# Moving the residual add of the combine stage from VectorE to GpSimd in an attention and mixture-of-experts kernel

## The chip, the cores and the metric

The kernel runs on one core of a Trainium2 chip. The metric is the device time of one execution in microseconds. Engines are called TensorE (PE in the profile, its weight load PEld), VectorE (DVE), ScalarE (ACT), GpSimd (POOL) and SyncE (SP, which here only issues DMAs).

## What is computed

One transformer layer on x of 4 x 2048 tokens by 512 features, float32:

```python
x = x + layernorm(attention(layernorm(x)))   # linear attention, 16 heads, random features
x = x + layernorm(ffn(layernorm(x)))         # 32 experts, 4 per token, plus a shared expert
```

The last line is where the change lies. For a token, ffn is the weighted sum of its experts' outputs plus the output of a shared expert, `silu(X @ sw1.T) * (X @ sw3.T) @ sw2.T`. That sum is normalised over the 512 features (mean 0, variance 1, epsilon 1e-5) and the residual, the x of the line above, is added.

## The kernel before

The 8192 tokens are worked on in NG = 16 groups of G = 512; a group is held as a tile of 128 partitions by A = 4 by 512 features. The stages follow each other: projection, sums over the sequence, attention with routing, experts, combine. The last three are in one block of programs (attend_route_and_expert_stage, line 1728), each engine with an instruction stream of its own, in order, tied to the others by semaphores. The change is in expert_and_combine_programs (line 1292).

**Experts.** For each of 32 experts GpSimd gathers rows by indirect DMA (L1412), TensorE turns them and does the two layers, VectorE weighs the result, and GpSimd adds it by indirect DMA into the sum acc in HBM (L1426).

**Combine.** It begins when the last of those additions has landed. The groups are taken in a written order, of which the text calls the places positions 0 to 15:

```python
ORDER = (2, 3, 4, 0, 5, 6, 7, 1, 8, 9, 10, 11, 12, 13, 14, 15)   # line 1301
```

Groups 0 and 1 (positions 3 and 7) had their shared expert done before the experts, so they have no matmuls here. For the others TensorE does, per group, up of the next group (L1485: two halves i, each eight matmuls into gates and eight into ups, 128x512) and then down of this group in four passes a (L1500, four matmuls each). Up of a half waits until VectorE has read the banks before (h_ready); down's first pass waits for both halves of low (low_ready); down's pass a waits until VectorE has taken the product of pass a-2 out of its PSUM bank (y_copied).

VectorE's order in a group at position q with matmuls (lines 1693 to 1721) is: make_shift of q-1 (L1663, waits for rstd_ready), hidden of the next group's half 0 (L1610: silu'd gate, from SBUF, times up, from PSUM), include 0 (L1642: down's product, from PSUM, plus the loaded sum, from SBUF), hidden half 1, measure 0 (L1651: statistics of one 128x512 tile), include 1, low half 0 (L1615: h minus its 16-bit part, both from SBUF), measure 1, include 2, low half 1, measure 2, include 3, **add of q-1 (L1670)**, measure 3, aggregate (L1656). At positions 3 and 7 it is make_shift, four measures, add, aggregate. "The first include" of a group is L1642 with a = 0.

ScalarE's order at q: silu of the next group's two halves (L1540), make_high of half 0 (L1546), scale of q-1 (L1552: four activations that normalise the sum in place, after the shift), make_high of half 1, store of q-1 (L1559, a DMA that waits for out_ready). GpSimd only makes rstd for each position: it adds epsilon (L1436) when the aggregate is there, and raises to the power -0.5 (L1438).

SyncE loads: load_acc of q (L1361) into one of ACCS = 5 buffers, where from q = 5 it waits for out_ready of q-5; load_x1 (L1354) into one of X1S = 5 buffers after their store; load_shared (L1348) after up of an earlier group.

add(q) waits for z_ready (scale of q done) and x1_loaded, adds the whole tile in one instruction of 128x2048, x1 + total into x1, and counts out_ready, for which the store and load_acc wait.

Elsewhere in the kernel, the profile's lines name L329 and L330 (memsets on GpSimd in the projection), L1251 and L1253 (GpSimd's add of epsilon and power in the attention stage), L1105 and L1101 (VectorE, 128x2048, both inputs in SBUF, in the attention stage).

Of the kernel before, what the change touches and what calls it, by code (L numbers as in the profile page):

```python
# [14 lines left out]
NG = T // G  # L15
# [12 lines left out]
ALU = mybir.AluOpType  # L28
# [1263 lines left out]
def expert_and_combine_programs(nc, io, keep, t, wait_routed, wait_slots):  # L1292

    with ExitStack() as tiles:
# [3 lines left out]
        XTS, X1S, ACCS = 8, 5, 5  # L1298
# [13 lines left out]
        x1 = [t.sb(f"x1{r}", [P, A, E]) for r in range(X1S)]  # L1312
        total = [y[0][:], y[1][:]] + [r[:].rearrange("p a n -> p (a n)").bitcast(F32).rearrange(
            "p (a e) -> p a e", a=A) for r in rows]
# [13 lines left out]
        x1_loaded, out_stored = ([t.sem(f"{n}{r}") for r in range(X1S)] for n in ("x1_loaded", "out_stored"))  # L1328
# [4 lines left out]
        stats_ready, mv_ready, var_ready, rstd_ready, shift_ready, z_ready, out_ready, power_ready = (  # L1333
            t.sem(n) for n in ("stats_ready", "mv_ready", "var_ready", "rstd_ready", "shift_ready", "z_ready",
                               "out_ready", "power_ready"))
# [67 lines left out]
        def pool_program(pool):  # L1403
            def gather(e):
                r = e % AHEAD
                pool.wait_ge(slot_loaded[e % RING], 16 * (e // RING) + 16)
                if e >= AHEAD:
                    pool.wait_ge(turned_ready, A * (e - AHEAD + 1))
                for a in range(A):
                    if e < AHEAD:  # L1410
                        pool.wait_ge(cleared, A * e + a + 1)
                    nc.gpsimd.indirect_dma_start(  # L1412
                        out=rows[r][:, a, :], out_offset=None, in_=io["rows"],
                        in_offset=bass.IndirectOffsetOnAxis(ap=slot[e % RING][:, a, 0:1], axis=0),
                        bounds_check=T - 1, oob_is_err=False).then_inc(gathered[r], 16)

            def add(e):

                if e == 0:
                    for k in range(2):  # L1420
                        pool.wait_ge(y_stored[k], 16 * NS // 2)
                if e >= 1:
                    pool.wait_ge(added[1 - e % 2], 16 * A * ((e - 1) // 2 + 1))
                for a in range(A):
                    pool.wait_ge(y_copied, A * (NS + e) + a + 1)
                    nc.gpsimd.indirect_dma_start(  # L1426
                        out=io["acc"],
                        out_offset=bass.IndirectOffsetOnAxis(ap=slot[e % RING][:, a, 0:1], axis=0),
                        in_=y[e % 2][:, a, :], in_offset=None, bounds_check=T + CAP - 1, oob_is_err=True,
                        compute_op=ALU.add).then_inc(added[e % 2], 16)  # L1430

            def make_rstd(n):
                pool.wait_ge(mv_ready, n + 1)
                if n >= 1:
                    pool.wait_ge(z_ready, n)
                nc.gpsimd.tensor_scalar(rstd[:], mv[:, :, 1], 1e-5, None, ALU.add).then_inc(var_ready, 1)  # L1436
                pool.wait_ge(var_ready, n + 1)
                nc.gpsimd.tensor_tensor(rstd[:], rstd[:], power[:], ALU.pow).then_inc(rstd_ready, 1)  # L1438

            for e in range(AHEAD):  # L1440
                gather(e)
            nc.gpsimd.memset(power[:], -0.5).then_inc(power_ready, 1)
            pool.wait_ge(power_ready, 1)
            for e in range(NE):
                if e + AHEAD < NE:
                    gather(e + AHEAD)
                add(e)
            for k in range(2):
                pool.wait_ge(added[k], 16 * A * NE // 2)
            for n in range(NG):  # L1450
                make_rstd(n)

        def pe_program(pe):
# [150 lines left out]
        def dve_program(dve):  # L1604
            def hidden(e, i):
                dve.wait_ge(gate_ready, IC * e + i + 1)
                if e >= 1:
                    dve.wait_ge(high_ready, IC * (e - 1) + i + 1)
                    dve.wait_ge(low_ready, IC * (e - 1) + i + 1)
                nc.vector.scalar_tensor_tensor(out=h[i][:], in0=gate[i][:], scalar=H_SCALE, in1=ups[i][:],  # L1610
                                               op0=ALU.mult, op1=ALU.mult).then_inc(h_ready, 1)

            def low(e, i):
                dve.wait_ge(high_ready, IC * e + i + 1)
                nc.vector.tensor_tensor(parts[e % 2][:, i, 1, :], h[i][:], parts[e % 2][:, i, 0, :],  # L1615
                                        ALU.subtract).then_inc(low_ready, 1)
# [21 lines left out]
            def include(q, a):  # L1638
                n, at = ORDER[q], total[q % ACCS][:, a, :]
                dve.wait_ge(acc_loaded[q % ACCS], 16 * (q // ACCS) + 16)  # L1640
                dve.wait_ge(y_ready, A * (NE + n) + a + 1)
                nc.vector.scalar_tensor_tensor(out=at, in0=ys[a % 2][:], scalar=1.0 / H_SCALE, in1=at, op0=ALU.mult,  # L1642
                                               op1=ALU.add).then_inc(y_copied, 1)

            def measure(q, a):
                n = ORDER[q]
                if n >= NS:
                    dve.wait_ge(y_copied, A * (NE + n) + a + 1)
                else:
                    dve.wait_ge(acc_loaded[q % ACCS], 16 * (q // ACCS) + 16)  # L1650
                nc.vector.bn_stats(stats[:, a, :], total[q % ACCS][:, a, :]).then_inc(stats_ready, 1)  # L1651

            def aggregate(q):
                dve.wait_ge(stats_ready, A * (q + 1))
                for a in range(A):
                    ins = nc.vector.bn_aggr(mv[:, a, :], stats[:, a, :])  # L1656
                ins.then_inc(mv_ready, 1)

            def make_shift(q):
                dve.wait_ge(rstd_ready, q + 1)  # L1660
                if q >= 1:
                    dve.wait_ge(z_ready, q)
                nc.vector.scalar_tensor_tensor(out=shift[:], in0=mv[:, :, 0], scalar=-1.0, in1=rstd[:], op0=ALU.mult,  # L1663
                                               op1=ALU.mult).then_inc(shift_ready, 1)

            def add(q):
                r = q % X1S
                dve.wait_ge(z_ready, q + 1)
                dve.wait_ge(x1_loaded[r], 16 * (q // X1S) + 16)
                nc.vector.tensor_tensor(x1[r][:], x1[r][:], total[q % ACCS], ALU.add).then_inc(out_ready, 1)  # L1670

            wait_routed(dve)
# [20 lines left out]
            for q, n in enumerate(ORDER):  # L1693
                p = NE + n
                if q >= 1:
                    make_shift(q - 1)
                if n >= NS:
                    more = p + 1 < PASSES
                    if more:
                        hidden(p + 1, 0)  # L1700
                    include(q, 0)
                    if more:
                        hidden(p + 1, 1)
                    measure(q, 0)
                    include(q, 1)
                    if more:
                        low(p + 1, 0)
                    measure(q, 1)
                    include(q, 2)
                    if more:  # L1710
                        low(p + 1, 1)
                    measure(q, 2)
                    include(q, 3)
                    if q >= 1:
                        add(q - 1)
                    measure(q, 3)
                else:
                    for a in range(A):
                        measure(q, a)
                    add(q - 1)  # L1720
                aggregate(q)
            make_shift(NG - 1)
            add(NG - 1)

    return sp_program, pe_program, act_program, dve_program, pool_program


# [144 lines left out]
```

## Time and profile before

| | |
|---|---|
| time of three runs, us | 2137.11 median (2131.04, 2137.11, 2138.62) |
| profiled execution, span, us | 2130.7 (its first to its last instruction; the execution's own time is not given apart from it; the shortest run is 2131.04) |
| TensorE busy in the span | 1825.4 us, 86% |
| VectorE | 1207.3 us, 57% |
| ScalarE | 1124.4 us, 53% |
| GpSimd | 768.8 us, 36% |
| mean granted TensorE clock | 0.948 |
| combine stage | from about 1936 us to the end: 195 us, VectorE busy 147.6, TensorE 141.4, ScalarE 73.8, GpSimd 20.2 |
| residual adds L1670 | 16 of 128x2048, 2.28 us median |

The profile has one execution of the program. Busy time counts instructions of an engine; the timeline gives each instruction's start and duration, and behind it in brackets how long the engine was idle before and what released it. On VectorE durations overlap: an instruction starts before the record of the one before has ended. The clock is TensorE's granted clock as a share of 2.4 GHz.

### The profile page before, as it was taken

The page shows a single profiled execution, that of the slowest core. Times are in us where ns is not written, and L with a number is a line of the kernel's source. Part 1 is how long each engine was busy: PE and PEld are TensorE (multiplying, and loading weights), DVE is VectorE, ACT ScalarE, POOL GpSimd, SP SyncE. Part 2 cuts the span into 40 slices and gives each one's busy share as a digit, 9 for nine tenths or more (in the row PEclk, how much of TensorE's full clock was granted, in tenths as well). Part 3 has the DMA queues.
Part 4 walks back from the last instruction along what each step waited for, and adds up shares of the span by engine and source line. Part 5 has one row for each costly group of instructions (what it writes and reads, how often), then busy time and mean ns, then how long its engine had stood idle before and what let it go on. Part 6 is the DMA issues. An engine that isn't in the chain of part 4 may idle for free.

```text
span 2130.7 us, 33664 instructions
## 1 busy us (share of the span) xinstructions
PE 1825.4 (86%) x12931; PEld 890.0 (42%) x12976; DVE 1207.3 (57%) x2230; ACT 1124.4 (53%) x1371; POOL 768.8 (36%) x718
## 2 busy tenths in 40 slices
PE   8899999999978999699788887635998899997785
PEld 6444444444436788133233333312444444443332
DVE  7676667666650000158788888872444434445786
ACT  5554554555525666478677877422444444442343
POOL 0000000000000000024677788876677777761110
PEclk9999999999998999899999999857999999999997
DMA  7435353445328887568678765443789999987983
GB/s 255 150 116 197 105 182 131 149 164 183 121 97 213 209 214 191 132 166 230 186 241 234 227 206 193 159 183 100 164 194 222 244 232 243 220 150 231 330 301 138
DMA packets 188848, 405.15 MB, mean 190 GB/s; under 512 B 33812, under 2 KB 72084, under 8 KB 172064
## 3 DMA queue, kind: packets, MB, share of 16 engines
q1 hardware_dynamic: 83184, 222.41, 35.2%
q10 hardware_dynamic: 68640, 124.26, 16.7%
q0 software_dynamic: 36864, 56.32, 14.2%
q8 instruction: 103, 1.69, 0.3%
q14 instruction: 57, 0.47, 0.1%
HBM read 237.06 MB, written 177.08 MB: 194 GB/s over the span
## 4 chain that ended last, share of the span: by engine, by line
DVE 14%; PE 14%; DMA 10%; issue 8%; POOL 8%; ACT 4%; SPq 1%; POOLq 0%; DVEq 0%; ACTq 0%
POOL slot_dram L1260 4%; PE s_gates L1485 4%; PE s_ups L1485 3%; DMA s_rows<-rows_dram,s_slot 3%; PE s_ys L1500 3%; DMA acc_dram<-s_y,s_slot 3%; DMA s_spread<-share_dram 2%; ACT s_xT L1531 2%; PE s_turned L1462 1%; DMA den_dram<-s_den 1%; DVE s_heads L1101 1%; DVE s_stats L1651 1%; DVE s_x L1670 1%; POOL acc_dram L1426 1%; DMA s_dens<-den_dram 1%
## 5 line engine op out<-in xcount | busy, mean ns | idle before, releaser
L258 PE MATMUL s_proj<-s_xT,keep_wqkv 128*128 128x512 f16 x1536 | 341.8, 380 | 0.0
L1260 POOL DMA_INDIRECT slot_dram<-keep_filled,keep_slots x256 | 301.7, 1179 | 95.2 <-issue 73.8
L1426 POOL DMA_INDIRECT acc_dram<-s_y,s_slot x128 | 203.0, 1586 | 93.5 <-issue 34.2
L898 PE MATMUL s_y<-keep_wo,s_at_hl 128*128 128x512 f16 x768 | 191.0, 402 | 44.9 <-ACT s_z L988 44.8
L258 PEld LDWEIGHTS s_proj<-s_xT,keep_wqkv 128*128 128x128 f16 x1536 | 147.6, 98 | 183.4 <-issue 12.6
L237 PE MATMUL s_proj<-keep_wqkv,s_xT 128*128 128x512 f16 x768 | 179.5, 393 | 34.5 <-ACT s_xT L500 34.5
L1540 ACT ACTIVATE s_gate<-s_gates 128x512 f32<-128x512 f32 x96 | 57.1, 597 | 262.5 <-PE s_ups L1485 217.0
L339 POOL TENSOR_SCALAR s_rstd<-s_mv 128x4 f32<-128x4 f32 x16 | 16.0, 998 | 494.8 <-DVE s_mv L354 494.8
L1610 DVE SCALAR_TENSOR_TENSOR s_h<-s_gate,s_ups 128x512 f32<-128x512 f32 x96 | 65.9, 687 | 213.2 <-ACT s_gate L1540 213.1
L518 ACT ACTIVATE s_hl<-s_rot 128x1024 f16<-128x1024 f32 x64 | 67.6, 1057 | 221.0 <-DVE s_rot L400 220.5
L676 ACT ACTIVATE s_phi<-s_logits 128x1024 f32<-128x1024 f32 x128 | 131.0, 1023 | 85.1 <-PE s_logits L697 85.1
L387 DVE TENSOR_TENSOR s_by_cos<-s_proj,s_table 128x1024 f32<-128x1024 f32 x64 | 78.4, 1224 | 171.2 <-PE s_proj L258 171.2
L967 ACT ACTIVATE s_phi<-s_logits 128x1024 f32<-128x1024 f32 x128 | 131.0, 1024 | 47.4 <-PE s_logits L867 46.5
L1531 ACT ACTIVATE s_xT<-s_turned 128x1024 f16<-128x1024 f16 x128 | 125.0, 1018 | 44.8 <-PE s_turned L1462 44.7
L898 PEld LDWEIGHTS s_y<-keep_wo,s_at_hl 128*128 128x128 f16 x768 | 73.1, 102 | 180.0 <-ACT s_z L988 57.7
L1412 POOL DMA_INDIRECT s_rows<-rows_dram,s_slot x128 | 132.8, 1037 | 42.7 <-issue 31.1
L737 PE MATMUL s_parts<-s_phi,s_v 128*33 128x128 f32 x2048 | 138.9, 278 | 2.5 <-DMA s_v<-v_dram 2.1
L1485 PE MATMUL s_gates<-s_xT,s_w 128*128 128x512 f16 x512 | 124.4, 387 | 9.9 <-ACT s_xT L1531 9.9
L237 PEld LDWEIGHTS s_proj<-keep_wqkv,s_xT 128*128 128x128 f16 x768 | 75.2, 100 | 131.8 <-ACT s_xT L500 42.2
L1500 PE MATMUL s_ys<-s_w,s_parts 128*128 128x512 bf16 x480 | 125.5, 383 | 5.1 <-DVE s_y L1627 3.5
L1485 PE MATMUL s_ups<-s_xT,s_w 128*128 128x512 f16 x512 | 121.2, 380 | 0.0
L1627 DVE TENSOR_SCALAR s_y<-s_ys,s_slot 128x512 f32<-128x512 f32 x128 | 93.8, 748 | 44.9 <-PE s_ys L1500 44.6
(165 smaller groups left out, 3207.4 us busy)
## 6 DMA issues: line engine op xcount, KB each, us to landing
s_x<-x_in SPq DMA_DIRECT2D x32, 1024.0 KB, 9.7
qk_dram<-s_hl ACTq DMA_DIRECT2D x32, 1024.0 KB, 5.9
keep_ahead<-qk_dram SPq DMA_DIRECT2D x48, 512.0 KB
acc_dram<-s_zero SPq DMA_DIRECT2D x17, 1024.0 KB, 11.5
v_dram<-s_v ACTq DMA_DIRECT2D x16, 1056.0 KB
s_v<-v_dram SPq DMA_DIRECT2D x16, 1056.0 KB, 10.8
s_spread<-share_dram SPq DMA_DIRECT2D x64, 256.0 KB
x_dram<-s_x ACTq DMA_DIRECT2D x16, 1024.0 KB, 5.2
```

Source lines behind the costliest of these rows:

```text
L237: mm = nc.tensor.matmul(proj[half][:, 512 * b:512 * b + 512], left, right, start=(c == 0 and i == 0), stop=(c == EC - 1 and i == 2))
L258: mm = nc.tensor.matmul(out[:, 512 * b:512 * b + 512], left, right, start=(c == 0 and i == 0), stop=(c == EC - 1 and i == 2))
L676: nc.scalar.activation(phi[n % 2][:].rearrange("p h m -> p (h m)"), logits[n % 2][:], ACT.Exp, scale=1.0 / M_SCALE).then_inc(phi_ready, 1)
L737: mm = nc.tensor.matmul(parts[ch % 2][at:at + D + 1, h // 2 * M:(h // 2 + 1) * M], v[n % 2][:, a * H + h, :], phi[half][:, h % HALF, :], s ...
L898: mm = nc.tensor.matmul(y[m % 2][:], at_hl[n % 2][:, s, c, a * P:(a + 1) * P], keep["wo"][:, w, c, :], start=(c == 0 and i == 0), stop=(c ...
L967: nc.scalar.activation(phi[m % PHIS][:].rearrange("p h q -> p (h q)"), logits[:], ACT.Exp, scale=1.0 / M_SCALE).then_inc(phi_ready, 1)
L1260: nc.gpsimd.indirect_dma_start(out=io["slot"], out_offset=bass.IndirectOffsetOnAxis(ap=slots[n % 2][:, a * K + j:a * K + j + 1], axis=0), ...
L1412: nc.gpsimd.indirect_dma_start(out=rows[r][:, a, :], out_offset=None, in_=io["rows"], in_offset=bass.IndirectOffsetOnAxis(ap=slot[e % RING ...
L1426: nc.gpsimd.indirect_dma_start(out=io["acc"], out_offset=bass.IndirectOffsetOnAxis(ap=slot[e % RING][:, a, 0:1], axis=0), in_=y[e % 2][:, ...
L1485: mm = nc.tensor.matmul(bank[:], w[:, c, i * P:(i + 1) * P], left[:, s, c, :], start=(c == 0 and s == 0), stop=(c == EC - 1 and s == 1))
L1500: mm = nc.tensor.matmul(ys[a % 2][:], parts[p % 2][:, i, s, a * P:(a + 1) * P], w[:, i, :], start=(i == 0 and s == 0), stop=(i == IC - 1 a ...
L1531: nc.scalar.activation(xT[k][:, :, :, a * P:(a + 1) * P], turned[a % 2][:].bitcast(F16).rearrange("p (s c q) -> p s c q", s=2, c=EC), ACT. ...
```

## The change

GpSimd gets add_residual(q), with the waits and the operands that VectorE's add(q) had, and runs it for the position before ahead of make_rstd of each position from 1 on. VectorE's add(q-1) is taken out of both kinds of group; what stays is add_last for the last position, with a wait for the fifteen earlier adds.

```diff
--- before.py
+++ after.py
@@ -1437,6 +1437,12 @@
                 pool.wait_ge(var_ready, n + 1)
                 nc.gpsimd.tensor_tensor(rstd[:], rstd[:], power[:], ALU.pow).then_inc(rstd_ready, 1)
 
+            def add_residual(q):
+                r = q % X1S
+                pool.wait_ge(z_ready, q + 1)
+                pool.wait_ge(x1_loaded[r], 16 * (q // X1S) + 16)
+                nc.gpsimd.tensor_tensor(x1[r][:], x1[r][:], total[q % ACCS], ALU.add).then_inc(out_ready, 1)
+
             for e in range(AHEAD):
                 gather(e)
             nc.gpsimd.memset(power[:], -0.5).then_inc(power_ready, 1)
@@ -1448,6 +1454,8 @@
             for k in range(2):
                 pool.wait_ge(added[k], 16 * A * NE // 2)
             for n in range(NG):
+                if n >= 1:
+                    add_residual(n - 1)
                 make_rstd(n)
 
         def pe_program(pe):
@@ -1663,10 +1671,12 @@
                 nc.vector.scalar_tensor_tensor(out=shift[:], in0=mv[:, :, 0], scalar=-1.0, in1=rstd[:], op0=ALU.mult,
                                                op1=ALU.mult).then_inc(shift_ready, 1)
 
-            def add(q):
+            def add_last():
+                q = NG - 1
                 r = q % X1S
                 dve.wait_ge(z_ready, q + 1)
                 dve.wait_ge(x1_loaded[r], 16 * (q // X1S) + 16)
+                dve.wait_ge(out_ready, q)
                 nc.vector.tensor_tensor(x1[r][:], x1[r][:], total[q % ACCS], ALU.add).then_inc(out_ready, 1)
 
             wait_routed(dve)
@@ -1711,16 +1721,13 @@
                         low(p + 1, 1)
                     measure(q, 2)
                     include(q, 3)
-                    if q >= 1:
-                        add(q - 1)
                     measure(q, 3)
                 else:
                     for a in range(A):
                         measure(q, a)
-                    add(q - 1)
                 aggregate(q)
             make_shift(NG - 1)
-            add(NG - 1)
+            add_last()
 
     return sp_program, pe_program, act_program, dve_program, pool_program
```

## Rows read from the trace of the kernel before

**Rows 1.** Busy time by stretch: us; busy PE, PEld, DVE, ACT, POOL; PEclk, DMA, GB/s

```profile
2052.06:2097.89 45.83, 42.49 (x191) 18.11 (x193) 39.82 (x74) 20.66 (x32) 5.06 (x8) 1.00 0.69 243
```

**Rows 2.** Timeline of a steady group: start us, us, engine, line, operation, idle before

```profile
2051.46 0.69 DVE L1610 SCALAR_TENSOR_TENSOR s_h<-s_gate,s_ups 128x512 f32<-128x512 f32 x1
2052.06 0.69 DVE L1642 SCALAR_TENSOR_TENSOR s_y<-s_ys,s_y 128x512 f32<-128x512 f32 x1
2052.72 2.92 ACT L1552 ACTIVATE s_rows<-s_rows,s_shift,s_rstd 128x512 f32<-128x512 f32 x4
2053.86 0.68 DVE L1642 SCALAR_TENSOR_TENSOR s_y<-s_ys,s_y 128x512 f32<-128x512 f32 x1
2056.24 0.69 DVE L1615 TENSOR_TENSOR s_parts<-s_h,s_parts 128x512 f16<-128x512 f32 x1
2058.03 2.29 DVE L1670 TENSOR_TENSOR s_x<-s_x,s_rows 128x2048 f32<-128x2048 f32 x1
2060.96 0.38 DVE L1656 BATCH_NORM_AGGREGATE s_mv<-s_stats 128x2 f32<-128x6 f32 x4
2061.43 0.23 POOL L1436 TENSOR_SCALAR s_rstd<-s_mv 128x4 f32<-128x4 f32 x1 [10.11 <-DVE s_mv L1656]
2062.16 1.61 PEld L1500 LDWEIGHTS s_ys<-s_sw,s_parts 128*128 128x128 f16 x8
2062.80 0.16 DVE L1663 SCALAR_TENSOR_TENSOR s_shift<-s_mv,s_rstd 128x4 f32<-128x4 f32 x1 [1.47 <-POOL s_rstd L1438]
2063.52 0.68 DVE L1642 SCALAR_TENSOR_TENSOR s_y<-s_ys,s_y 128x512 f32<-128x512 f32 x1
...
2097.89 0.68 DVE L1642 SCALAR_TENSOR_TENSOR s_rows<-s_ys,s_rows 128x512 f32<-128x512 f32 x1
```

**Rows 3.** Groups of instructions, GpSimd's memsets: busy us, mean ns, idle before

```profile
L329 POOL MEMSET s_zero<- 128x512 f32 x1 | 0.5, 524 | 0.0
L330 POOL MEMSET s_v<- 128x64 f32 x1 | 0.2, 210 | 0.0
```

**Rows 4.** Timeline, attention stage: GpSimd's add behind a VectorE instruction

```profile
924.76 2.26 DVE L1105 TENSOR_TENSOR s_at_hl<-s_heads,s_at_hl 128x2048 f16<-128x2048 f32 x1
924.93 2.15 POOL L1251 TENSOR_TENSOR s_rstd<-s_mv,s_eps 128x2 f32<-128x2 f32 x1 [5.47 <-DVE s_mv L1140]
```

**Rows 5.** Timeline, attention stage: GpSimd's power ahead of a VectorE instruction

```profile
943.01 0.69 POOL L1253 TENSOR_TENSOR s_rstd<-s_rstd,s_power 128x2 f32<-128x2 f32 x1
943.56 2.29 DVE L1101 TENSOR_TENSOR s_heads<-s_heads,s_spread 128x2048 f32<-128x2048 f32 x1 [0.90 <-DMA s_spread<-share_dram]
```

**Rows 6.** Timeline: first includes, scale and add at positions 1, 3, 4, 5, 8, 9

```profile
1954.64 0.69 DVE L1642 SCALAR_TENSOR_TENSOR s_y<-s_ys,s_y 128x512 f32<-128x512 f32 x1 [3.07 <-PE s_ys L1500]
1954.72 2.92 ACT L1552 ACTIVATE s_y<-s_y,s_shift,s_rstd 128x512 f32<-128x512 f32 x4
...
1977.04 2.93 ACT L1552 ACTIVATE s_rows<-s_rows,s_shift,s_rstd 128x512 f32<-128x512 f32 x4 [6.85 <-DVE s_shift L1663]
1980.00 2.29 DVE L1670 TENSOR_TENSOR s_x<-s_x,s_rows 128x2048 f32<-128x2048 f32 x1 [0.62 <-ACT s_rows L1552]
1984.77 0.68 DVE L1642 SCALAR_TENSOR_TENSOR s_rows<-s_ys,s_rows 128x512 f32<-128x512 f32 x1
...
1998.28 0.69 DVE L1642 SCALAR_TENSOR_TENSOR s_y<-s_ys,s_y 128x512 f32<-128x512 f32 x1 [1.97 <-PE s_ys L1500]
...
2028.41 0.69 DVE L1642 SCALAR_TENSOR_TENSOR s_rows<-s_ys,s_rows 128x512 f32<-128x512 f32 x1
...
2040.60 0.69 DVE L1642 SCALAR_TENSOR_TENSOR s_rows<-s_ys,s_rows 128x512 f32<-128x512 f32 x1 [0.65 <-PE s_ys L1500]
```

**Rows 7.** Timeline: shifts of positions 14 and 15, scale of position 14

```profile
2108.62 0.16 DVE L1663 SCALAR_TENSOR_TENSOR s_shift<-s_mv,s_rstd 128x4 f32<-128x4 f32 x1 [1.47 <-POOL s_rstd L1438]
2108.82 2.93 ACT L1552 ACTIVATE s_rows<-s_rows,s_shift,s_rstd 128x512 f32<-128x512 f32 x4 [6.85 <-DVE s_shift L1663]
2118.53 0.16 DVE L1663 SCALAR_TENSOR_TENSOR s_shift<-s_mv,s_rstd 128x4 f32<-128x4 f32 x1 [1.47 <-POOL s_rstd L1438]
```

## Prediction

> **What bounds the kernel now.** I read the table of busy time first. In four steady groups of the combine stage TensorE is busy 42.49 of 45.83 us at a granted clock of 1.00, VectorE 39.82, GpSimd 5.06 [rows 1]. Two engines are nearly full, so the share says only that neither is alone in charge. The order of instructions decides, and I read that next, in the timeline.
>
> Let t be the start of the first include (L1642) of a group. The same start in the next group is 11.46 us later, and from 2052.06 to 2097.89 there are four such steps of 11.46 [rows 2]. Two loops close in that time:
> - VectorE: twelve 128x512 operations start 0.60 us apart (L1610 to L1642, 2051.46 to 2052.06), the residual's add takes 2.20 of the engine, then L1651, the aggregate at t+8.90, GpSimd's L1436 at t+9.37, the shift at t+10.74, L1610, the next include at t+11.46. VectorE is idle only for the 1.47 us in which GpSimd makes rstd.
> - TensorE: down's fourth pass needs the second include (t+1.80); behind it come the 32 matmuls of the next group, and the weight load of the next down is at t+10.10. Its product is ready for the include 1.36 us later: t+11.46.
>
> So the loops tie. Taking 2.20 us from VectorE shortens the first loop and leaves the second as it is. **The most a steady group can win is nothing that I can see**; gains are open only where TensorE isn't in the loop: the two groups without matmuls (positions 3 and 7, groups 0 and 1) and the end.
>
> **The change, part by part.**
>
> Removed: fifteen adds on VectorE, of 2.29 us each (2.20 of the engine). Kept there: the last one, after the last scale; its new wait for fifteen earlier adds costs nothing, since the GpSimd add of group 14 lies before the rstd on which that last scale rests.
>
> Added on GpSimd: fifteen adds of 128x2048 f32, two inputs from SBUF, one output. GpSimd does nothing like it in the kernel before. What streams on it is memset: 128x512 in 524 ns, 128x64 in 210 ns [rows 3], so 0.70 ns a column over some 0.17 us. **Lower end**: one pass of 2048 columns, 1.6 us. The add moves three operands; if one port carries them in turn, 3 x 2048 x 0.70 + 0.17 = 4.5 us. **Upper end**: twice that, 9 us, if its loop doesn't keep a memset's pace. I take 4.5. The Trainium skill (GPSIMD Engine Reference, "Performance versus the Vector engine") gives 4497 ns for this very operation and size; by it the sum would be the one below.
>
> Moved on GpSimd: the add of the group before stands ahead of the rstd, which so waits for it. Scale starts at t+0.66 and takes 2.92; GpSimd takes 0.09 us from a finished neighbour to its start (2060.96 + 0.38 to 2061.43) [rows 2]. The add begins at t+3.67 and ends at t+8.17. The rstd was due at t+9.37, so its queue costs nothing in a steady group. ScalarE's store, and the silu behind it, waited for the add's end at t+8.26 (2058.03 + 2.29) and now wait until t+8.17: no change. SyncE's load of a sum waits for the same semaphore, for a buffer needed four groups later: nothing. No DMA is added and no DMA queue gets more instructions.
>
> **What it does to VectorE.** In the attention stage GpSimd's add of 128x2, of some 0.2 us, took 2.15 us when it began behind a VectorE instruction with both inputs in SBUF (924.76, 2.26 us), and ended 0.06 us after it [rows 4]. So one of the two is kept out while the other reads. For the other order the rows have only short reads: a VectorE instruction with two SBUF inputs began inside GpSimd's power (943.01 to 943.70) and took its usual 2.29 [rows 5]; but that power reads two columns, and the rest of its time is arithmetic. Bounds: VectorE is not held at all (0), or it is held to the end of the add. I take the second, since it is the mirror of rows 4 and the add reads until near its end.
>
> The Trainium skill (SBUF — State Buffer, "Who interferes with whom") says the pair of ports is locked by whoever begins first, for the whole instruction, against VectorE instructions with two SBUF inputs. Rows 4 agree; rows 5 don't show "whole instruction"; no row has a long GpSimd read. Taken literally it gives the hold that I sum.
>
> Which VectorE instructions have two SBUF inputs here? L1610 and L1642 take one from PSUM, L1651 takes one. Only the two L1615 remain, and the second is due at t+4.18 (2056.24) [rows 2], **0.5 us after GpSimd's add begins**. It is held until t+8.17: 3.99 us lost, 2.20 won, all behind it (L1651, two includes, the aggregate, rstd, shift) 1.8 us later. Period 13.25 instead of 11.46, and in that period the add again begins at t+3.67. TensorE needs the held result only at t+10.10.
>
> The sum, by positions in the order of groups (starts in [rows 6], the end in [rows 7]):
> - 1: scale began 0.08 us behind the include, the add comes 0.58 earlier: 3.4 - 2.2 = +1.2
> - 2, 5, 6, 9 to 14 (nine groups): 9 x 1.8 = +16.2
> - 3, 7: the add is in the chain. Before, from the end of scale (1979.97) to GpSimd's rstd lay 0.03, the add's 2.20 and the aggregate's 0.47 (2060.96 to 2061.43), 2.7 in all; now 0.09 + 4.5 + 0.05 (taken as half the 0.09, since no other engine is asked): +1.9 each, +3.8
> - 4: TensorE restarted slowly after its pause and the step was already 13.51 (1984.77 to 1998.28): 0
> - 8: the step was 12.19 (2028.41 to 2040.60), now 13.25: +1.1
> - 15: from shift to shift 9.91 before (2108.62 to 2118.53); now 0.20 to scale's start, then 2.93 + 0.09 + 4.5 + 0.05 + 1.37 = 9.1: -0.8
>
> Together **+21.5 us**. The profiled execution spans 2130.7, close to the fastest run shown (2131.04); against the median of 2137.11 the forecast is 2158.6. Each 0.5 us on the add is about 7 us on the sum: 4.0 gives 2151, 5.0 gives 2166.
>
> **Rivals.**
> 1. *The add holds nobody* (the end on the other side), or it comes just behind the second L1615, 0.5 us away, and does its hold in idle ground. For it: rows 5. Against: rows 4. Then the steady groups stay on TensorE's 11.46; before positions 3 and 7 the rstd comes at t+8.2 instead of t+9.37 (-1.2) and inside them +1.9, so +0.7 each; the end wins 1.2 and 0.8. Sum about -1 to -2: 2135.6. It decides as soon as L1615 isn't held past t+6.4.
> 2. *A short add*, two passes or one: 3.0 us leaves a hold of 2.5 against 2.2 won, sum within 1 us of zero; 1.6 us gives both groups without matmuls and the end their 2 to 3 us each, about -10: 2127. For it: memset's pace is one pass. Against: three operands.
> 3. *A long add*, above 5.7 us: scale, add and rstd become a loop of their own (t+3.67, the add, 0.05, 1.37, 0.7 to the next include: 5.8 + add), even without a hold. At 9 us it is 14.8 a group, +50 us, with the hold +88: 2187 to 2225.
> 4. *The hold is wider*: if the includes (one input from PSUM, one from SBUF) are held too, one more operation is behind it, 0.6 us a group, +7: 2166. It lies inside the forecast's own range.
>
> **Chances.** The forecast 0.60 (with rival 4), rival 1 0.24, a short add 0.07, a long add 0.09. A measurement of this kernel tells 0.5% (10.7 us) from no change. Of the forecast's share a tenth lies under that bound (an add under 3.85 us): slower 0.54 + 0.09 = 0.63. Same: 0.06 + 0.24 + 0.04 = 0.34. Faster by over 0.5% needs the add at one pass and no hold: 0.03. The forecast's own range is 2148 to 2169. Cases of both signs: the range for 8 in 10 reaches down to rival 1, 2133, and up to 2168; the long add and the shortest stay outside.
>
> **What would show it.** Right: GpSimd adds near 4.5 us, starting 3.7 us behind the first include; in each group one L1615 whose end is at the add's end (a long record, or an idle gap before it), a step of 13.2 between first includes, VectorE without its 2.29 us add, TensorE with gaps of 2 us ahead of its third down. The steps of positions 3 and 7 longer by 1.9. Wrong: steps of 11.46 with L1615 at 0.69 (rival 1), or L1436 starting just at the end of an add in steady groups (rival 3). The forecast also falls if TensorE's granted clock, 1.00 in rows 1, sinks under the longer gaps: a slow restart in each group would give the 13.51 of position 4, little more than 13.25, but half the clock throughout would give far more.

## The result, and the profile after

The changed kernel takes 2158.56 us (median of 4 runs, 2156.28 to 2166.05) against 2137.86 (4 runs of the kernel before, 2131.04 to 2139.08): ratio 1.0105, 95% interval 1.0078 to 1.0132, about 1% slower. Forecast: 2158.6. That the two agree to a tenth of a microsecond is luck: single runs of the changed kernel lie 10 us apart, the sum was 0.9 us too high (the table below) and the median from which it was counted, 2137.11, 0.75 us too low.

Line numbers have moved: the first lines named below are L1444 (GpSimd's add, new), L1623 (low, L1615 before), L1650 (include, L1642), L1659 (statistics), L1664 (aggregate), L1671 (shift, L1663), L1680 (the last add).

Busy time of each engine on the page of the kernel after:

```profile
span 2154.5 us, 33664 instructions
PE 1839.0 (85%) x12931; PEld 894.3 (42%) x12976; DVE 1220.4 (57%) x2215; ACT 1123.7 (52%) x1371; POOL 839.3 (39%) x733
```

From the first include of position 0 (1941.84 before, 1945.01 after) to the start of the last add (2121.68 and 2145.48) it is 179.84 us before and 200.47 after: **+20.6 us, the whole of the loss**. The 3.2 us by which the combine stage begins later lie in stages that the change doesn't touch; single runs of the kernel before differ by more than that.

Groups of instructions in the combine stage (busy us, mean ns, idle before):

```profile
L1623 DVE TENSOR_TENSOR s_parts<-s_h,s_parts 128x512 f16<-128x512 f32 x26 | 63.2, 2431 | 0.0
L1444 POOL TENSOR_TENSOR s_x<-s_x,s_rows 128x2048 f32<-128x2048 f32 x9 | 40.6, 4506 | 37.2 <-ACT s_rows L1560 37.2
```

The 26 lows took 17.7 us before; now they take 63.2, and one GpSimd add takes 4.51 us. A steady group in the timeline (start us, us, engine, line), against [rows 2]:

```profile
2081.09 0.68 DVE L1650 SCALAR_TENSOR_TENSOR s_y<-s_ys,s_y 128x512 f32<-128x512 f32 x1
2081.74 2.92 ACT L1560 ACTIVATE s_y<-s_y,s_shift,s_rstd 128x512 f32<-128x512 f32 x4
2083.48 0.68 DVE L1623 TENSOR_TENSOR s_parts<-s_h,s_parts 128x512 f16<-128x512 f32 x1
2084.73 4.52 POOL L1444 TENSOR_TENSOR s_x<-s_x,s_y 128x2048 f32<-128x2048 f32 x1 [4.39 <-ACT s_y L1560]
2085.27 4.53 DVE L1623 TENSOR_TENSOR s_parts<-s_h,s_parts 128x512 f16<-128x512 f32 x1
2089.72 0.68 DVE L1659 BATCH_NORM_STATS2 s_stats<-s_y 128x6 f32<-128x512 f32 x1
2089.84 0.60 ACT L1548 ACTIVATE s_gate<-s_gates 128x512 f32<-128x512 f32 x1 [4.67 <-POOL s_x L1444]
2091.19 1.61 PEld L1508 LDWEIGHTS s_ys<-s_sw,s_parts 128*128 128x128 f16 x8
2091.76 0.38 DVE L1664 BATCH_NORM_AGGREGATE s_mv<-s_stats 128x2 f32<-128x6 f32 x4
2092.23 0.23 POOL L1436 TENSOR_SCALAR s_rstd<-s_mv 128x4 f32<-128x4 f32 x1 [2.98 <-DVE s_mv L1664]
2093.61 0.16 DVE L1671 SCALAR_TENSOR_TENSOR s_shift<-s_mv,s_rstd 128x4 f32<-128x4 f32 x1 [1.47 <-POOL s_rstd L1438]
2094.32 0.68 DVE L1650 SCALAR_TENSOR_TENSOR s_rows<-s_ys,s_rows 128x512 f32<-128x512 f32 x1
```

Take the first include, 2081.09, as t. The add begins at t+3.64. The second low is issued at t+4.18, as before, and its record is 4.53 us long, 3.85 more than usual: it ends at 2089.80, 0.55 us behind GpSimd's end (2084.73 + 4.52 = 2089.25); a low's own time is 0.68. The next statistics start at 2089.72. TensorE's weight load (2091.19) is at t+10.10, as in [rows 2]; its product could have been used at 2092.55, and the include comes at 2094.32. GpSimd's L1436 waited 2.98 us for VectorE, not for its own queue. The step is 13.23 instead of 11.46.

Four of these steps in the table by stretch (columns as in [rows 1]):

```profile
2067.87:2120.78 52.91, 45.54 (x189) 18.92 (x192) 46.76 (x70) 20.66 (x32) 23.11 (x12) 0.94 0.59 200
```

VectorE is busy 46.76 of 52.91 us, more than with its own adds (39.82 of 45.83), since a held instruction counts as busy.

Position 3, against [rows 6]: the include of position 2, then the chain from shift to shift.

```profile
1970.45 0.68 DVE L1650 SCALAR_TENSOR_TENSOR s_rows<-s_ys,s_rows 128x512 f32<-128x512 f32 x1
...
1982.95 0.16 DVE L1671 SCALAR_TENSOR_TENSOR s_shift<-s_mv,s_rstd 128x4 f32<-128x4 f32 x1 [1.47 <-POOL s_rstd L1438]
1986.16 4.49 POOL L1444 TENSOR_TENSOR s_x<-s_x,s_rows 128x2048 f32<-128x2048 f32 x1 [3.24 <-ACT s_rows L1560]
1990.62 0.23 POOL L1436 TENSOR_SCALAR s_rstd<-s_mv 128x4 f32<-128x4 f32 x1
1992.00 0.16 DVE L1671 SCALAR_TENSOR_TENSOR s_shift<-s_mv,s_rstd 128x4 f32<-128x4 f32 x1 [6.09 <-POOL s_rstd L1438]
1992.71 0.68 DVE L1650 SCALAR_TENSOR_TENSOR s_rows<-s_ys,s_rows 128x512 f32<-128x512 f32 x1
```

From shift to shift 9.05 us where it was 7.21: the rstd starts as the add ends (1986.16 + 4.49 to 1990.62). The end, against [rows 7]:

```profile
2133.27 0.16 DVE L1671 SCALAR_TENSOR_TENSOR s_shift<-s_mv,s_rstd 128x4 f32<-128x4 f32 x1 [1.47 <-POOL s_rstd L1438]
2136.47 4.50 POOL L1444 TENSOR_TENSOR s_x<-s_x,s_rows 128x2048 f32<-128x2048 f32 x1 [3.24 <-ACT s_rows L1560]
2136.82 0.69 DVE L1659 BATCH_NORM_STATS2 s_stats<-s_y 128x6 f32<-128x512 f32 x1
2137.80 0.69 DVE L1650 SCALAR_TENSOR_TENSOR s_y<-s_ys,s_y 128x512 f32<-128x512 f32 x1 [0.29 <-PE s_ys L1508]
2140.94 0.23 POOL L1436 TENSOR_SCALAR s_rstd<-s_mv 128x4 f32<-128x4 f32 x1
2142.33 0.16 DVE L1671 SCALAR_TENSOR_TENSOR s_shift<-s_mv,s_rstd 128x4 f32<-128x4 f32 x1 [2.69 <-POOL s_rstd L1438]
```

From shift to shift 9.06 us where it was 9.91. During this add VectorE ran statistics (2136.82) and an include with one input from PSUM and one from SBUF (2137.80), both at their usual 0.69: they aren't held.

All steps between first includes, us (a step over positions 3 or 7 covers two groups), and the last from the include of position 15 to the last add:

| step from position | before | after | difference | forecast |
|---|---|---|---|---|
| 0 to 1 | 12.80 | 12.79 | 0.0 | 0 |
| 1 to 2 | 11.46 | 12.65 | +1.2 | +1.2 |
| 2 to 4 | 18.67 | 22.26 | +3.6 | +3.7 |
| 4 to 5 | 13.51 | 13.22 | -0.3 | 0 |
| 5 to 6 | 11.46 | 13.21 | +1.8 | +1.8 |
| 6 to 8 | 18.67 | 22.27 | +3.6 | +3.7 |
| 8 to 9 | 12.19 | 13.23 | +1.0 | +1.1 |
| 9 to 14, five steps | 57.29 | 66.14 | +8.9 | +9.0 |
| 14 to 15 | 10.81 | 12.57 | +1.8 | +1.8 |
| 15 to the last add | 12.98 | 12.13 | -0.8 | -0.8 |
| sum | 179.84 | 200.47 | +20.6 | +21.5 |

### The profile page after: what moved, and what is told of

The parts are those of the page before. It is cut to its first block, busy times and chain, and to the rows that moved or that the text cites. A ratio compares the mean times of both kernels' runs of the same rounds, so it can differ in the third digit from the quotient of the medians.

```text
span 2154.5 us, 33664 instructions
## 1 busy us (share of the span) xinstructions
PE 1839.0 (85%) x12931; PEld 894.3 (42%) x12976; DVE 1220.4 (57%) x2215; ACT 1123.7 (52%) x1371; POOL 839.3 (39%) x733
## 4 chain that ended last, share of the span: by engine, by line
DVE 14%; PE 12%; DMA 11%; issue 10%; POOL 8%; ACT 4%; SPq 1%; POOLq 0%; DVEq 0%; ACTq 0%
PE s_gates L1493 4%; POOL slot_dram L1260 3%; PE s_ups L1493 3%; DMA acc_dram<-s_y,s_slot 3%; DMA s_spread<-share_dram 2%; PE s_ys L1508 2%; ACT s_xT L1539 2%; DMA s_rows<-rows_dram,s_slot 2%; DVE s_stats L1659 2%; DMA den_dram<-s_den 1%; DVE s_heads L1101 1%; PE s_turned L1470 1%; POOL acc_dram L1426 1%; DMA s_dens<-den_dram 1%; DVE s_at_hl L1105 1%
## 5 line engine op out<-in xcount | busy, mean ns | idle before, releaser
L1260 POOL DMA_INDIRECT slot_dram<-keep_filled,keep_slots x256 | 308.3, 1204 | 94.3 <-issue 71.8
L898 PE MATMUL s_y<-keep_wo,s_at_hl 128*128 128x512 f16 x768 | 196.1, 410 | 46.3 <-ACT s_z L988 46.3
L1623 DVE TENSOR_TENSOR s_parts<-s_h,s_parts 128x512 f16<-128x512 f32 x96 | 111.9, 1166 | 48.7 <-ACT s_parts L1554 48.7
L1493 PE MATMUL s_gates<-s_xT,s_w 128*128 128x512 f16 x512 | 124.3, 387 | 10.8 <-ACT s_xT L1539 10.8
```

The source lines that it names most:

```text
L898: mm = nc.tensor.matmul(y[m % 2][:], at_hl[n % 2][:, s, c, a * P:(a + 1) * P], keep["wo"][:, w, c, :], start=(c == 0 and i == 0), stop=(c ...
L1260: nc.gpsimd.indirect_dma_start(out=io["slot"], out_offset=bass.IndirectOffsetOnAxis(ap=slots[n % 2][:, a * K + j:a * K + j + 1], axis=0), ...
L1493: mm = nc.tensor.matmul(bank[:], w[:, c, i * P:(i + 1) * P], left[:, s, c, :], start=(c == 0 and s == 0), stop=(c == EC - 1 and s == 1))
```

## The experiments

That the sum fits doesn't show that each term is what it was called. Three claims were put to the test: the loss is the low held by the add (and not GpSimd's queue, or its traffic); what holds it is a GpSimd instruction that reads; and a steady group had nothing to win, because VectorE's and TensorE's loops tied. Each ratio is the time over that of the kernel before, run on the same chip, with its 95% interval in brackets. Where the interval holds 1, the time alone tells no difference, and the steps of the timeline decide; steady ones repeat to 0.02 us in most runs.

### The add behind the low (e1_after_low)

```diff
             def add_residual(q):
                 r = q % X1S
                 pool.wait_ge(z_ready, q + 1)
+                n = ORDER[q + 1]
+                if NS <= n < NG - 1:
+                    pool.wait_ge(low_ready, IC * (NE + n + 2))
```

> Edit: GpSimd's add also waits until VectorE has done both lows of the next group, so it begins behind the second low and meets no VectorE instruction with two SBUF inputs before the shift. Theory (the loss of a steady group is the low held to the end of the add): every low back at 0.69 us; add from t+4.9 to t+9.4, rstd, shift at t+10.8, step between first includes about 11.5 instead of 13.22. Positions 3 and 7 keep their longer chain (each +1.9), the end keeps -0.8: about +4 us on the kernel before. Rival A (the loss is GpSimd's queue: rstd behind the add): the add begins 1.2 us later, so steps grow to 14.4, about +30. Rival B (GpSimd's traffic slows VectorE's instructions whatever their inputs): includes and statistics longer than 0.69 during the add, steps stay at 12 or more, +10 or more.

Ratio 1.0017 (0.9992 to 1.0042): +4 us, with 0 inside the interval. The steps and the end add up to +3.8. A step of the timeline (its low is L1626, the add L1447, the aggregate L1667):

```profile
2067.58 0.68 DVE L1653 SCALAR_TENSOR_TENSOR s_y<-s_ys,s_y 128x512 f32<-128x512 f32 x1
2071.76 0.68 DVE L1626 TENSOR_TENSOR s_parts<-s_h,s_parts 128x512 f16<-128x512 f32 x1
2072.58 4.51 POOL L1447 TENSOR_TENSOR s_x<-s_x,s_y 128x2048 f32<-128x2048 f32 x1 [5.74 <-issue]
2074.40 0.38 DVE L1667 BATCH_NORM_AGGREGATE s_mv<-s_stats 128x2 f32<-128x6 f32 x4
2077.06 0.22 POOL L1436 TENSOR_SCALAR s_rstd<-s_mv 128x4 f32<-128x4 f32 x1
2078.44 0.16 DVE L1674 SCALAR_TENSOR_TENSOR s_shift<-s_mv,s_rstd 128x4 f32<-128x4 f32 x1 [3.65 <-POOL s_rstd L1438]
2079.15 0.68 DVE L1653 SCALAR_TENSOR_TENSOR s_rows<-s_ys,s_rows 128x512 f32<-128x512 f32 x1
```

The low is back at 0.68, the add begins 5.0 us behind the first include instead of 3.64, and the step is 11.57 (one of 11.87 among them). Positions 3 and 7 have the same 9.05 from shift to shift and the end the same 9.06 as after. Rival A wanted 14.4, rival B 12 or more; both fall as the cause of the loss in a steady group. VectorE now stands 3.65 us idle ahead of the shift: here it is GpSimd's chain (low, add, rstd) that gives 11.57.

### The add in four pieces (e2_four_pieces)

```diff
-                nc.gpsimd.tensor_tensor(x1[r][:], x1[r][:], total[q % ACCS], ALU.add).then_inc(out_ready, 1)
+                for a in range(A):
+                    ins = nc.gpsimd.tensor_tensor(x1[r][:, a, :], x1[r][:, a, :], total[q % ACCS][:, a, :], ALU.add)
+                ins.then_inc(out_ready, 1)
```

> Edit: the changed kernel, with GpSimd's add cut into four instructions of 128x512. Theory (the ports are held for one instruction): a piece takes about 1.25 us, the low waits at most for the piece that runs and gets in behind it, 0.7 to 1.9 us instead of 4.5; steps about 11.5 to 11.8, about +5 us on the kernel before. Rival (the next piece is queued and goes first): low held through all four, about 5 us in all, steps 13.7, +28 us.

Ratio 1.0016 (0.9995 to 1.0036): about +3 us, with 0 inside the interval; steady steps 11.45. From the timeline, the include, GpSimd's first piece, the low, the second piece:

```profile
2065.13 0.69 DVE L1652 SCALAR_TENSOR_TENSOR s_y<-s_ys,s_y 128x512 f32<-128x512 f32 x1 [0.84 <-PE s_ys L1510]
...
2068.20 1.27 POOL L1445 TENSOR_TENSOR s_x<-s_x,s_y 128x512 f32<-128x512 f32 x1 [4.75 <-ACT s_y L1562]
...
2069.32 0.70 DVE L1625 TENSOR_TENSOR s_parts<-s_h,s_parts 128x512 f16<-128x512 f32 x1
...
2069.43 1.72 POOL L1445 TENSOR_TENSOR s_x<-s_x,s_y 128x512 f32<-128x512 f32 x1
```

A piece takes 1.27 us. The low comes 0.15 us before the first piece ends, goes in between, and the second piece is the one that waits (1.72 us). Of 26 lows 24 are at 0.68 to 0.71. That most of them wait for nothing is in part a matter of where they fall. The two at 1.28, behind the positions without matmuls, show the rule: they come in the middle of a piece, wait 0.6 us, and still go ahead of the next one. So the ports change hands between instructions, and the rival (28 us) falls. At positions 3 and 7 four pieces cost more than one (9.47 from shift to shift). The include at 2065.13 shows 0.84 us of waiting for TensorE: with the hold gone the steady step is TensorE's.

### GpSimd writes only (e4_writes_only)

The kernel before with this ahead of make_rstd, `idle[0]` a tile that is free in this stage:

```diff
+                if n >= 1:
+                    pool.wait_ge(z_ready, n)
+                    for k in range(3):
+                        nc.gpsimd.memset(idle[0], 0.0).then_inc(idle_ready, 1)
+                        pool.wait_ge(idle_ready, 3 * (n - 1) + k + 1)
```

> Edit: the kernel before, and at the place of the moved add GpSimd does three memsets of 128x2048 (about 1.6 us each), which read nothing. Theory (only GpSimd's reads hold VectorE out): lows stay at 0.69 us, steady steps 11.46; at positions 3 and 7 the rstd comes some 2.2 us later behind the memsets: about +4 us. Rival (any long GpSimd instruction holds it): the second low held for 1.1 us or more in each group, steps of 12.6 or more, +15 us or more.

The single run took 2144.25 us; the kernel before took 2125.82 to 2141.79 on this chip (median 2132.42). From the first include to the last add it is 6.8 us longer than before, forecast about 4. Groups of the combine stage:

```profile
L1455 POOL MEMSET s_xT<- 128x2048 f32 x45 | 81.2, 1805 | 67.7 <-ACT s_rows L1558 38.0 <-ACT s_y L1558 28.0
L1621 DVE TENSOR_TENSOR s_parts<-s_h,s_parts 128x512 f16<-128x512 f32 x26 | 17.7, 680 | 0.0
```

Three memsets fill 5.5 us from the end of the scale, more than the add's 4.5, and the lows stay at 0.68. VectorE's own adds, with two SBUF inputs and wholly inside the memsets in a steady group (2080.75 in 2078.40 to 2083.93), stay at 2.28 to 2.29 us too. Steps are 11.52, the 0.06 being GpSimd's own chain (scale, memsets, rstd); the steps over positions 3 and 7 are 21.70, +3.0 where about 2.2 was forecast, since a memset took 1.8 us and not 1.6. A GpSimd that only writes doesn't hold the low.

### GpSimd reads one input (e8_one_input)

The same place, with `nc.gpsimd.tensor_scalar(idle[1], idle[0], 1.0, None, ALU.add)` twice.

> Edit: the kernel before, and at the place of the moved add GpSimd does two tensor_scalar of 128x2048 with one input from SBUF, to spare tiles. Theory (GpSimd's reads hold VectorE's instructions with two SBUF inputs, however many operands GpSimd reads): the second low is held to the end of the first of them, 1.0 to 2.5 us longer than 0.69 or, if the next goes first, to the end of the second; VectorE's add is still there, so steps grow by the whole hold: 12.5 to 14.5. Rival (only a GpSimd instruction with two inputs holds it): lows at 0.69, steps 11.5.

Steps are 18.63, the whole 2255.62 us (a single run; 2140.17 the median of the kernel before). The kind was right, the size not. GpSimd's first instruction, the low, VectorE's add, GpSimd's second:

```profile
2063.70 5.37 POOL L1455 TENSOR_SCALAR s_xT<-s_xT 128x2048 f32<-128x2048 f32 x1 [4.40 <-ACT s_y L1558]
...
2064.24 3.66 DVE L1621 TENSOR_TENSOR s_parts<-s_h,s_parts 128x512 f16<-128x512 f32 x1
...
2069.01 2.27 DVE L1676 TENSOR_TENSOR s_x<-s_x,s_y 128x2048 f32<-128x2048 f32 x1
...
2069.16 7.35 POOL L1455 TENSOR_SCALAR s_xT<-s_xT 128x2048 f32<-128x2048 f32 x1
```

The low is held, 3.66 us, 2.98 more than usual where 1.0 to 2.5 was forecast: one input is enough. But this instruction takes 5.37 us, more than the two-input add, and two of them make GpSimd's chain the loop (scale's end + 5.37 + 7.35 + rstd), which I hadn't priced. The rows show two more things. The second takes 7.35 us, since VectorE's add, begun 0.15 us earlier, kept it out for 2.0, as in [rows 4]. And the low ended 1.2 us before GpSimd's first one did, so the hold was over 1.8 us before that instruction's end; in the kernel after it lasted to 0.1 us before the add's end.

### No add at all (e3_no_add)

The kernel before, with VectorE's add cut to `x1[r][:, 0, 0:4]`.

> Edit: the kernel before, with VectorE's add cut to four columns of one tile; the output lacks the residual sum elsewhere. It shows what taking the add from VectorE could give at the very most. Theory (VectorE's and TensorE's loops tie): steps of steady groups stay at 11.46; positions 3 and 7 lose 2.2 each twice (18.67 to about 14.3) and the end loses some 6.6: about -15 us. Rival (VectorE alone sets the steady step): steps of 10.4 or less, about -25 us or more.

Ratio 0.9942 (0.9912 to 0.9972), -12 us, forecast -15. The seven steady steps are 11.45, as with the add. What shrinks is the steps over positions 3 and 7 (18.67 to 14.47), the step from 4 (13.51 to 12.44) and the end (10.81 to 8.76 and 12.98 to 10.89). So with VectorE's order as it was, there was no gain to be had in a steady group, whoever does the add.

### Order and place, one at a time and together (e5_deferred, e7_reorder_only, e6_both)

e5_deferred makes the rstd first and adds behind the shift:

```diff
             for n in range(NG):
-                if n >= 1:
-                    add_residual(n - 1)
                 make_rstd(n)
+                if 1 <= n < NG - 1:
+                    pool.wait_ge(shift_ready, n + 1)
+                    add_residual(n - 1)
...
-                if q >= 1:
-                    store(q - 1)
+                if q >= 2:
+                    store(q - 2)
             scale(NG - 1)
+            store(NG - 2)
...
-            add_last()
+            add_late(NG - 2)
+            add_late(NG - 1)
```

> Edit: GpSimd makes rstd of a position first and adds the residual of the position before it behind the shift (store one position later); the adds of positions 14 and 15 are on VectorE, the first of them in the time of the last scale. Theory (hold plus a TensorE loop of 11.46): the add runs from the shift to 1.7 us behind the first include and ends before the first low, so lows stay at 0.69; steady steps stay at 11.45 although VectorE has lost its add; the gain lies at positions 3 and 7 (18.67 to about 15.3) and the end (about -4): -11 us on the kernel before. Rival (VectorE sets the steady step once the hold is gone): steps 9.5 to 10.5, -20 us or more.

Ratio 0.9944 (0.9927 to 0.9961), -12 us. Steady steps 11.45, over positions 3 and 7 15.51, as expected. Not as expected: at positions 4 and 8 the first low is still held, since there the include comes 0.7 us behind the shift (1987.71), where in a steady group VectorE waits for TensorE and it comes 2.8 us behind (the include, then the low):

```profile
1988.43 0.69 DVE L1652 SCALAR_TENSOR_TENSOR s_rows<-s_ys,s_rows 128x512 f32<-128x512 f32 x1
1990.82 2.22 DVE L1625 TENSOR_TENSOR s_parts<-s_h,s_parts 128x512 f16<-128x512 f32 x1
```

What it costs isn't shown: the step from position 4 is 13.33, against 13.51 before and 12.44 in e3_no_add, and that from 8 is 11.98, against 12.19 and 12.03. A third one, at position 9, is 1.17 us long.

e7_reorder_only is the kernel before with this order of VectorE's (the adds stay on it):

```diff
                     include(q, 0)
+                    include(q, 1)
                     if more:
                         hidden(p + 1, 1)
                     measure(q, 0)
-                    include(q, 1)
+                    measure(q, 1)
                     if more:
                         low(p + 1, 0)
-                    measure(q, 1)
                     include(q, 2)
                     if more:
                         low(p + 1, 1)
-                    measure(q, 2)
                     include(q, 3)
+                    measure(q, 2)
```

> Edit: the kernel before with the new order of VectorE's instructions alone; the adds stay on VectorE. Theory (both loops are 11.46): TensorE's loop is shorter, VectorE's is not, steps stay at 11.46, within 2 us of the kernel before. Rival (TensorE alone sets the step): steps 10.8, -6 us or more.

Ratio 1.0004 (0.9982 to 1.0025); steady steps, taken between shifts, 11.46, as forecast.

e6_both is both edits:

> Edit: as e5_deferred, and VectorE takes the second include directly behind the first, with its hidden and statistics after them. Theory (TensorE's loop runs over hidden and measure between the two includes): the fourth down pass starts 1.2 us earlier, steps of positions 9 to 13 about 10.8 where e5_deferred has 11.45; in positions 4 to 8, where transfers are near their limit, perhaps less; -15 to -17 us on the kernel before. Rival (TensorE's loop is bound elsewhere): 11.45 as e5_deferred.

Ratio **0.9911** (0.9887 to 0.9935), -19 us, steady steps 10.53; the forecast was -15 to -17 and 10.8. Neither edit alone moves a steady step; together they take 0.93 us from each. Four steps by stretch, of e5_deferred and of e6_both (columns as in [rows 1]):

```profile
2052.15:2097.95 45.80, 42.47 (x191) 18.10 (x193) 31.74 (x69) 20.20 (x33) 23.70 (x13) 1.00 0.77 270
```

```profile
2050.74:2092.85 42.11, 41.79 (x191) 18.13 (x193) 31.75 (x69) 20.20 (x33) 23.27 (x13) 1.00 0.87 290
```

VectorE's work is the same, 31.7 us in four groups. TensorE was busy 42.47 of 45.80 us and is now busy 41.79 of 42.11, 99%: the pause in its loop is gone. That pause is this one, ahead of down's fourth pass, while VectorE comes to the second include (kernel before; e5_deferred has the same 0.75):

```profile
2066.05 1.04 PE L1500 MATMUL s_ys<-s_sw,s_parts 128*128 128x512 bf16 x4 [0.75 <-DVE s_y L1642]
```

So 10.53 us is TensorE's own work but for 0.08 us a group (41.79 / 4 = 10.45), and another order of VectorE's has next to nothing left to win there. e6_both beats both kernels.

## Why the prediction was right

- *The ceiling.* "the loops tie" held: without any add the steady step is 11.45, with the new order alone 11.46, with both changed 10.53. One count in it is off without effect: up to the add eleven 128x512 operations start 0.60 us apart, and the twelfth is the L1651 behind it.
- *The add's price.* Taken as 4.5 us from memset's pace times three operands; measured 4.51. The number held, but by luck as far as it came from that picture. The memset of 128x2048 took 1.80 us in e4_writes_only, not 1.6; worked out from it and the 524 ns of 128x512, three operands give about 5.2 us (an estimate), and the sum would have been some 10 us higher. And the one-input tensor_scalar took 5.37 us, so counting operands is no rule. The Trainium skill (GPSIMD Engine Reference, "Performance versus the Vector engine") has 4497 ns for this operation and size, and the trace agrees.
- *The queue.* The rstd waited for VectorE, not for the add, in steady groups: right. At positions 3 and 7 it waited for the add: +1.84 each against 1.9.
- *The hold.* Forecast 3.99 us on the second low, measured 3.85 (4.53 less 0.68); the add behind the low takes it away. This was the disputed step, and rows 4, which show the other order of the two instructions, were the right ones to go by. The Trainium skill (SBUF — State Buffer, "Who interferes with whom") names the same pairs, and the runs agree pair by pair: both inputs in SBUF against a reading GpSimd held, against a writing one not, one input from PSUM not held. The page's words "for the whole instruction", which it has beside VectorE's two-port modes, fit the add here and not the tensor_scalar.
- *Single terms off.* The sum is 0.9 us too high: 0.3 of it at position 4, where I kept 13.51 for a slow restart of TensorE and the step was 13.22, that of any held group; the rest is at most 0.15 a row of the table. The 13.51 is no fixed cost: the same step is 12.09 in e4_writes_only and 12.60 in e1_after_low.
- *The rivals.* Rival 1 (nobody held): the lows decide against it. Its second form, an add that comes just behind the low, is what e1_after_low is, at +4 us. Its sum was wrong: its own terms (twice +0.7, -1.2, -0.8) give -0.6 and not -1 to -2, and e1_after_low has 11.57 in a steady group where it took 11.46, and 9.06 at the end as the changed kernel. Rival 2 and 3: the add is 4.51. Rival 4 (includes held too): not held at 2137.80.

What isn't settled: why the low was free 1.8 us before the tensor_scalar's end and only 0.1 us before the add's.

## What to carry to other kernels

Before moving work off a nearly full engine, write out every loop that closes in one step; here two tied at 11.46 us, and relief of one was worth nothing until the order of the other was changed too. In these runs a long GpSimd instruction that reads SBUF (128x2048, 4.5 or 5.4 us) held VectorE's instructions with two SBUF inputs, and the reverse; those with one were not held. What counts is which instructions start in its span, so place it where there are none, or cut it into pieces. When both loops were opened, TensorE's own work (10.53 us) was the next bound. A neighbour 0.5 us away decided 1.8 us in each group.

## What was not expected of the hardware

- GpSimd's tensor_scalar of 128x2048 f32 with one input takes 5.37 us, its tensor_tensor add of two inputs 4.51, its memset 1.81.
- In the kernel after, the granted clock over four steady steps was 0.94 instead of 1.00, with gaps of up to 1.8 us ahead of TensorE's third down pass; TensorE was busy 45.54 us for the work that took 42.49. It cost nothing: TensorE had 1.8 us to spare in each step, and the steps are 13.22 to 13.24 all the same, that of 2081.09 among them, in which the clock was 1.00.
